# Two mixture-of-experts stages: index columns used where they lie, and two moved waits and reads

## The reference

```
# first experts: 8 experts, 256 hidden, the 2 best per token
topk_w, topk_idx = top_k(softmax(xf @ gate_w.T), 2)
for e in range(8):
    h = silu(xf @ w1[e].T) * (xf @ w3[e].T)
    out = out + gate_full[:, e:e + 1] * (h @ w2[e].T)

# second experts: 8 experts, 684 hidden, biases, the 2 farthest centroids
for e in range(8):
    h = silu(xs @ Wg[e] + bg[e]) * (xs @ W1[e] + b1[e])
    out = out + we[:, e:e + 1] * (h @ W2[e] + b2[e])
```

## Time and profile before

| | us |
|---|---|
| timed runs, median (lowest to highest) | 2411.94 (2408.89 to 2412.17) |
| the profiled execution's own time | 2414.36 |
| its span | 2412.6 |
| PE busy | 2079.7 (86%) |
| DVE busy | 1389.4 (58%) |
| ACT busy | 1534.8 (64%) |
| POOL busy | 440.3 (18%) |

### The profile page before, as it was taken

The page is one execution under the profiler, slowest core; times in us unless marked ns, Lnnn a source line. Parts: engine busy times, 40 slices in busy tenths (PEclk is TensorE's granted clock), DMA queues, the critical chain, the costliest instruction groups (busy, mean ns, idle before and its releaser), DMA issues. The chain is left out here.

```text
span 2412.6 us, 43912 instructions
## 1 busy us (share of the span) xinstructions
PE 2079.7 (86%) x13329; PEld 971.6 (40%) x13330; DVE 1389.4 (58%) x2986; ACT 1534.8 (64%) x2495; POOL 440.3 (18%) x678
## 2 busy tenths in 40 slices
PE   5997799950996999999999999999853699999992
PEld 4785455530661222222222222222242476766761
DVE  5567444347786444444445555553156687777774
ACT  2215333223774999999999999999862344444441
POOL 0030366642000000000000000000000134343430
PEclk9998899975996999999999999999976799999996
DMA  5001344443100000000002222222255265555656
GB/s 194 1 1 70 105 148 146 142 144 140 38 24 1 1 1 1 1 1 1 1 19 71 71 71 71 71 71 71 83 180 164 98 178 175 173 176 170 175 168 231
DMA packets 139075, 220.11 MB, mean 91 GB/s; under 512 B 14080, under 2 KB 108464, under 8 KB 138944
## 3 DMA queue, kind: packets, MB, share of 16 engines
q1 hardware_dynamic: 124160, 176.96, 23.6%
q0 software_dynamic: 13632, 37.24, 4.7%
q10 hardware_dynamic: 1152, 4.19, 0.4%
HBM read 161.82 MB, written 52.20 MB: 89 GB/s over the span
## 5 line engine op out<-in xcount | busy, mean ns | idle before, releaser
L1800 ACT ACTIVATE at_pexp<-at_psS 128x1024 f32<-128x1024 f32 x1024 | 964.2, 1023 | 42.9 <-PE at_psS L1706 39.8
L1814 DVE TENSOR_REDUCE at_mx<-at_psM 128x1 f32<-128x512 f32 x474 | 327.5, 691 | 464.3 <-PE at_psM L1733 464.3
L1720 PE MATMUL at_psO<-at_pexp,at_vst 128*32 128x512 f32 x4096 | 546.4, 605 | 0.1
L1706 PE MATMUL at_psS<-l1c_QT,l1c_KT 64*128 64x512 f16 x2048 | 403.6, 387 | 14.4 <-issue 5.6
L1706 PEld LDWEIGHTS at_psS<-l1c_QT,l1c_KT 64*128 64x128 f16 x2048 | 99.4, 92 | 632.4 <-ACT at_pexp L1800 598.9
L2136 PE MATMUL ex_psH<-wide_wgu,ex_xT 128*128 x1278 | 259.9, 357 | 0.2 <-issue 0.2
L2207 DVE SCALAR_TENSOR_TENSOR ex_bias<-ex_psH,top_w_scale,ex_bias 128x456 f32<-128x456 f32 x213 | 147.4, 692 | 76.7 <-PE ex_psH L2136 63.8
L988 POOL DMA_INDIRECT expert_rows<-ex_y,ex_odx x142 | 140.3, 988 | 259.5 <-issue 181.3
L2180 ACT ACTIVATE ex_sg<-ex_bias 128x228 f32<-128x228 f32 x213 | 83.7, 393 | 152.1 <-DVE ex_bias L2207 152.1
L1733 PE MATMUL at_psM<-at_ksumT,l1c_QT 64*128 64x512 bf16 x474 | 179.1, 378 | 0.6
L2136 PEld LDWEIGHTS ex_psH<-wide_wgu,ex_xT 128*128 128x128 f16 x1278 | 124.5, 97 | 111.8 <-issue 3.6
(11 more groups left out here) (362 smaller groups left out, 2782.6 us busy)
## 6 DMA issues: line engine op xcount, KB each, us to landing
ex_bias<-in_L_ffn_bg SPq DMA_DIRECT2D x71, 342.0 KB
ex_bias<-in_L_ffn_b SPq DMA_DIRECT2D x71, 342.0 KB
ex_piece<-in_L_ffn_W SPq DMA_DIRECT2D x48, 228.0 KB, 2.6
l1c_KT<-in_L_ffn_W SPq DMA_DIRECT2D x32, 342.0 KB, 3.4
halves<-l1c_KT SPq DMA_DIRECT2D x32, 342.0 KB, 3.3
wide_wgu<-halves SPq DMA_DIRECT2D x8, 1368.0 KB
ex_b<-in_L_ffn_b SPq DMA_DIRECT2D x71, 128.0 KB
normed<-rt_area SPq DMA_DIRECT2D x16, 512.0 KB, 2.6
```

Of the source, the lines that this page charges most:

```text
L1706: mm = pe.matmul(psS[:, n, hh * BANK:(hh + 1) * BANK], keys(k.KT, p)[r, kt * P:(kt + 1) * P], keys(k.QT, p)[r, c * BANK:(c + 1) * BANK], s ...
L1720: mm = pe.matmul(psO[g * VW:(g + 1) * VW, y, :], vst[:, p % 2, hh, kt, :], pexp[:, (p * ST + step) % 3 * 2 + n, hh * BANK:(hh + 1) * BANK] ...
L1800: act.activation(pexp[:, u % 6, :], psS[:, u % 2, :], ACT.Exp, scale=D ** -0.5 / (QS * QS)).then_inc(raised, 1)
L1814: dve.tensor_reduce(mx[:, n:n + 1], psM[:, :], AX.X, ALU.max).then_inc(reduced, 1)
```

## The change

Three edits. In `slot_transfers`, for both expert stages, the copies of index columns, the tiles idx and odx and the semaphores `indexed` and `passed` go; the transfers take their indices from the columns of `tok` and `dst`, and the 71 tiles are written as straight code. In the second experts SP waits, before it issues the biases of tile 0 and of tile 1, until the gather of that tile has landed. In the first experts PE's two reads of expert numbers move from the places where the numbers are used to the top of each step, ahead of the wait for the gather.

```diff
-    for st in steps(pool, NTILE, 8, LAG):
-        if st.on(0):
-            t, g = st.tile(0), st.slot(0, GR)
-            st.again(pool, got[g], st.lap(0, GR) * 16)
-            st.again(pool, x_turned, t - GR + 1)
-            pool.tensor_copy(idx[:, g, :], k.tok[:, ds(t, 1)]).then_inc(indexed, 1)
-        if st.on(LAG):
-            t, j = st.tile(LAG), st.slot(LAG, 2)
-            st.again(pool, put[j], st.lap(LAG, 2) * 16)
-            pool.tensor_copy(odx[:, j, :], k.dst[:, ds(t, 1)]).then_inc(indexed, 1)
...
-        if st.on(0):
-            pool.wait_ge(indexed, count)
-            pool.sem_inc(passed, 1)
+    for at in range(NTILE + LAG):
+        if at < NTILE:
+            t, g = at, at % GR
+            if t >= GR:
+                pool.wait_ge(got[g], t // GR * 16)
+                pool.wait_ge(x_turned, t - GR + 1)
             pool.indirect_dma_start(xg[:, g, :], None, k.xn_d,
-                                    bass.IndirectOffsetOnAxis(idx[:, g, :], 0)).then_inc(got[g], 16)
-        if st.on(LAG):
-            pool.wait_ge(indexed, count)
+                                    bass.IndirectOffsetOnAxis(k.tok[:, t:t + 1].bitcast(U32), 0)).then_inc(got[g], 16)
+        if at >= LAG:
+            t, j = at - LAG, at % 2
+            if t >= 2:
+                pool.wait_ge(put[j], t // 2 * 16)
             pool.wait_ge(y_done, t + 1)
-            pool.sem_inc(passed, 1)
-            pool.indirect_dma_start(k.y_d, bass.IndirectOffsetOnAxis(odx[:, j, :], 0), y[:, j, :],
+            pool.indirect_dma_start(k.y_d, bass.IndirectOffsetOnAxis(k.dst[:, t:t + 1].bitcast(U32), 0), y[:, j, :],
                                     None).then_inc(put[j], 16)
...
 (experts0, tensor)
                 for st in steps(pe, NTILE, 8, 3):
+                    eh, ey = (pe.value_load(k.tile_expert[0:1, ds(st.tile(lag), 1)], min_val=0, max_val=E - 1)
+                              if st.on(lag) else None for lag in (1, 3))
                     if st.on(0):
...
-                        e = pe.value_load(k.tile_expert[0:1, ds(t, 1)], min_val=0, max_val=E - 1)
                         pe.wait_ge(x_out, t + 1)
...
 (experts1, sync)
                         e = sp.value_load(k.tile_expert[0:1, ds(t, 1)], min_val=0, max_val=E - 1)

+                        if isinstance(t, int) and t < BR:
+                            sp.wait_ge(got[t], 16)
                         st.again(sp, h_done, (t - BR + 1) * HG)
```

More of the change, by code:

```diff
@@ L954, in _, with slot_transfers @@
                 ser(dve.tensor_scalar(k.tok[:, :], k.dst[:, :], T - 1, None, ALU.bitwise_and))
-def slot_transfers(pool, k, idx, odx, xg, y, got, put, x_turned, y_done, indexed, passed):
+def slot_transfers(pool, k, xg, y, got, put, x_turned, y_done):
     LAG = GR + 2
-    for st in steps(pool, NTILE, 8, LAG):
-        if st.on(0):
-            t, g = st.tile(0), st.slot(0, GR)
-            st.again(pool, got[g], st.lap(0, GR) * 16)
-            st.again(pool, x_turned, t - GR + 1)
-            pool.tensor_copy(idx[:, g, :], k.tok[:, ds(t, 1)]).then_inc(indexed, 1)
-        if st.on(LAG):
-            t, j = st.tile(LAG), st.slot(LAG, 2)
-            st.again(pool, put[j], st.lap(LAG, 2) * 16)
-            pool.tensor_copy(odx[:, j, :], k.dst[:, ds(t, 1)]).then_inc(indexed, 1)
[L975 to L978, removed]
-        if st.on(0):
-            pool.wait_ge(indexed, count)
-            pool.sem_inc(passed, 1)
-            pool.indirect_dma_start(xg[:, g, :], None, k.xn_d,
-                                    bass.IndirectOffsetOnAxis(idx[:, g, :], 0)).then_inc(got[g], 16)
-        if st.on(LAG):
-            pool.wait_ge(indexed, count)
+    for at in range(NTILE + LAG):
[4 more added lines that the diff above has]
+                pool.wait_ge(x_turned, t - GR + 1)
+            pool.indirect_dma_start(xg[:, g, :], None, k.xn_d,
+                                    bass.IndirectOffsetOnAxis(k.tok[:, t:t + 1].bitcast(U32), 0)).then_inc(got[g], 16)
[3 more added lines that the diff above has]
+                pool.wait_ge(put[j], t // 2 * 16)
             pool.wait_ge(y_done, t + 1)
-            pool.sem_inc(passed, 1)
-            pool.indirect_dma_start(k.y_d, bass.IndirectOffsetOnAxis(odx[:, j, :], 0), y[:, j, :],
+            pool.indirect_dma_start(k.y_d, bass.IndirectOffsetOnAxis(k.dst[:, t:t + 1].bitcast(U32), 0), y[:, j, :],
                                     None).then_inc(put[j], 16)
@@ L996, in experts0 @@
     with Stage(nc, "ex0") as s:
-        idx, odx = s.sb("idx", [P, GR, 1], U32), s.sb("odx", [P, 2, 1], U32)
         xg = s.sb("xg", [P, GR, C])
@@ L1011, in experts0 @@
         got, put = s.sems("got", GR), s.sems("put", 2)
-        indexed, passed = s.sem("indexed"), s.sem("passed")
         AR = 4
@@ L1039, in _ @@
             def _(pool):
-                slot_transfers(pool, k, idx, odx, xg, y, got, put, x_turned, y_done, indexed, passed)
+                slot_transfers(pool, k, xg, y, got, put, x_turned, y_done)
             @block.tensor
@@ L1061, in _ @@
                             mm = pe.matmul(psH[:, j, :], xT[:, j, kk, :],
-                                           k.w13[:, ds(e, 1), kk, :].rearrange("p a c -> p (a c)"),
+                                           k.w13[:, ds(eh, 1), kk, :].rearrange("p a c -> p (a c)"),
                                            start=(kk == 0), stop=(kk == KC - 1))
@@ L1079, in _ @@
                             mm = pe.matmul(psY[:, j, 0:C], hT[:, j, kk, :],
-                                           k.w2[:, ds(e, 1), kk, :].rearrange("p a c -> p (a c)"),
+                                           k.w2[:, ds(ey, 1), kk, :].rearrange("p a c -> p (a c)"),
                                            start=(kk == 0), stop=(kk == KC - 1))
```

## The result

The changed kernel takes 2392.57 us (median of 4 runs, 2387.68 to 2395.45) against 2411.18 us (4 runs of before beside it): a ratio of 0.9922, 95% interval 0.9904 to 0.9940. That is 18.6 us less. The prediction was 30.7 us less, 2382 us; the measured time lies within its range of 2375 to 2396, but outside the likeliest case's own, 2376 to 2390. The gain is six tenths of the one forecast. One of the forecast's own signs of being wrong also came up: the first stage was to be at least 17 us shorter, and it is 12.1 us shorter.

What follows compares the result with a forecast made beforehand. GpSimd's queue of index copies and indirect transfers was taken to bound the first experts, PE the second. Savings 22.8 + 1.5 + 0.7 + 5.7 = 30.7 us gave 2382 us, range 2375 to 2396.

Steps and rivals of the forecast that it cites:

- likeliest case: Whole kernel: the forecast's own case, 2382 us, with its own range 2376 to 2390 and a chance of 68%.
- signs of being wrong: Forecast wrong if the first stage is not at least 17 us shorter or the second start gains under 2 us.
- GpSimd's queue bounded the first experts: First experts: index copies and indirect transfers set the 3.40 us tile; without copies the round is 2.58 us (2.29 to 3.07).
- 22.8 us for the steady tiles: First experts, 62 periods: reads hidden, every tile falls from 3.40 to 3.03 us, saving 22.8 us.
- The reads' place: First experts: reads at the top are hidden, giving tiles of 3.03 us (22.8 us saved); with 3.12 it is 17.2.
- Rival 1: First experts: both reads exposed, array runs dry at each tile; tile 3.43 us, 2404 us in all; chance 8%.
- rival 4: First experts: another wait comes up, such as y for its buffer's last put; tile 3.13 to 3.31, 2388 to 2399 us; 8%.
- rival 2: Second experts' start: late biases hold DVE's add and eat the gain, up to 3.7 us more, about 2386 us; chance 10%.
- rival 3: First experts: the 0.79 us gap belongs to any transfer with its own waits; round 3.56 us, 2416 us; chance 6%.
- The start and the tail of the first experts: First experts: first psH matmul 1.5 us sooner (bounds 0.3 and 2); last put gains 0.7 us.
- The second start: Second experts: biases wait for first gathers, psH 6.2 us sooner, 0.5 taken off; gain 5.7 us (bounds 2 and 7).
- Straight code on GpSimd: GpSimd's loop of 8 tiles becomes straight code; cost taken as nothing, with 0.45 us per tile to spare.

Runs made afterwards that it cites:

- h first: DVE multiplies h of a tile before scaling y of an older one, first experts: 2380.09 us on the changed kernel, 2409.77 us on the kernel before.
- no reads: Changed kernel with PE's matmuls of the first experts all using expert 0's weights and reading no expert number; output differs from the reference: 2379.49 us.

## Why the prediction was right, and where its size was off

**Right: GpSimd's queue bounded the first experts.** With the copies gone the round could be 0.97 + 0.30 + 0.99 + 0.30 = 2.56 us, and the tile fell to 3.25 by the transfers alone; as long as the copies are there, neither the reads nor h first change anything.

**The term that was mis-sized: 22.8 us for the steady tiles, measured 10.3** (210.67 us for 62 periods before, 200.39 after). The step that failed is "DVE's h releases the h transposes about 1.0 us into the tile, the psY instructions follow within 0.3, the two reads end at 2.5, and the array wants the next transposes at 3.03. So the reads should vanish". Measured in the tile that starts at 379.11: h ends at 1.22, the two reads take the queue from about 1.6 to 3.0, and the transposes start at 3.24. Three small errors add up to 0.5 us, the whole slack: h 0.2 later, 0.1 more up to the first read, and 1.4 us instead of 1.2 for the two reads. Of each read, the load takes 0.30 and one register operation 0.15 us. By themselves these would just have fitted. But the sum ends where the reads end, and the 0.2 us from there to the start of the transposes had no term in it.

The sum also started from a favourable tile. Its 1.0 us fits one tile of 3.03 us of the kernel before, the one at 286.70, where h ends 1.02 us into the tile; in the next it ends at 1.24:

```profile
287.31 0.41 DVE L1120 TENSOR_TENSOR ex_h<-ex_psH,ex_sg 128x256 f32<-128x256 f32 x1
...
290.56 0.41 DVE L1120 TENSOR_TENSOR ex_h<-ex_psH,ex_sg 128x256 f32<-128x256 f32 x1
```

From there up to 390 us it ends 1.10 us or later in every tile of the kernel before, and so it does from tile 8 on in the changed one, except behind a jump, where the transposes themselves are late (0.7). The reason is the order on DVE: h stands behind y, and y behind the end of psY, the last matmuls ahead of the tile's transposes. That closes a ring through PE's queue, which the sum walked only in part. The two experiments that shorten this ring at different links (no reads, h first) both reach 3.03, and the one without GpSimd's relief reaches nothing.

The Trainium skill ("DMA: Bandwidth & Descriptors", latency and other measured facts) gives a floor of about 600 ns for a load into a register; two of them would be 1.2 us, an estimate from that page. In this case's traces the load instruction itself takes 0.30 us, half of that floor; with the register operation, the check and the gaps one read holds the queue about 0.7 us, 1.4 for the two.

**Also short: a jump in the loop.** The prediction gave it no term. At a lead of 0.25 us it costs 0.5: a tile of 3.7 us instead of about 3.2. With h first, at a lead of 0.8, the tile at the jump takes 3.10 to 3.12 us instead of 3.03. Over the 62 periods the six jumps account for some 3 of the 12.5 us by which the steady tiles fell short.

**The reads' place: credited with up to 5.6 us, worth little.** The prediction read the tiles of 3.12 us as the cost of the reads' old places (22.8 against 17.2 us). With the reads back there 62 tiles of the changed kernel take 201.6 us instead of 200.4, and the medians differ by 2.1 us, which can't be told from nothing; nor can the gain of the move in the kernel before.

**The rivals.** Rival 1, the exposed reads, named the mechanism that came true but priced it at a tile of 3.43 and 2404 us; rival 4 had the tile (3.13 to 3.31) and the time (2388 to 2399) with another cause. So the time lies inside the range because that was drawn to take in rival 2 and most of rival 4, and not because the forecast's own case held in the first experts; to that extent it was luck. Rival 4's example, y waiting for its buffer's last put, ended only 2.5 us of DVE's waits before y between 300 and 480 us; psY ended the rest. The 2.5 us are one wait, in the tile from 456.88 to 460.69, the one of 3.81 us without a jump:

```profile
L1117 DVE TENSOR_SCALAR ex_y<-ex_psY,top_wgt 128x256 f32<-128x256 f32 x55 | 26.6, 483 | 103.2 <-PE ex_psY L1066 100.7 <-DMA expert_rows<-ex_y,top_dst 2.5
...
457.87 0.48 DVE L1117 TENSOR_SCALAR ex_y<-ex_psY,top_wgt 128x256 f32<-128x256 f32 x1 [2.47 <-DMA expert_rows<-ex_y,top_dst]
```

**Right: rival 3 is false.** A transfer with waits of its own starts 0.30 us behind another when what it waits for is done. The 0.79 us of the old gathers stood behind a semaphore that the copy had only just raised, and a put stands as long behind a y just written (380.00 to 380.79). No run has the copies without that wait, or GpSimd's old loop without the copies, so how the gain divides between them isn't shown.

**The start and the tail of the first experts.** The second gather and the first psH matmuls:

```profile
263.67 0.95 POOL L969 DMA_INDIRECT ex_xg<-normed,top_tok  x1 [0.31 <-issue]
...
269.43 3.62 PE L1049 MATMUL ex_psH<-l_w,ex_xT 128*128 x4
```

psH starts 9.2 us behind `top_tok` instead of 10.3: 1.1 gained of the 1.5 forecast. Half of that is gone by tile 8, since the ring already slows the first tiles, which ran at 3.03 to 3.12 before: tile 8 is 0.5 us sooner. From tile 70's transposes to the last put it is now 503.39 - 492.19 = 11.2 us against 12.5, 1.3 gained where 0.7 was forecast:

```profile
502.14 0.48 DVE L1117 TENSOR_SCALAR ex_y<-ex_psY,top_wgt 128x256 f32<-128x256 f32 x1 [1.02 <-DMA expert_rows<-ex_y,top_dst]
...
503.39 0.97 POOL L977 DMA_INDIRECT expert_rows<-ex_y,top_dst  x1 [0.53 <-issue]
```

In sum 0.5 + 10.3 + 1.3 = 12.1 us, the gain of the stage.

**The second start: forecast 5.7, measured 6.5 to 6.6.** Its steps held. The gathers landed in 3 us, psH started 7.0 us sooner (forecast 6.2), DVE's add waited for a bias pair that took 1900.06 - 1893.26 = 6.8 us (the 6.7 of the earlier trace rows), and 0.5 was given back. What was better is the first gather. With no copy ahead it starts 1.97 us behind `top_tok` instead of 2.74, 0.8 sooner where I had given it 0.3. Rival 2, the late biases, would have cost up to 3.7 us.

**Straight code on GpSimd** shows no cost: its transfers start 0.30 us behind one another or wait for DVE.

## What to carry to other kernels

When a queue that sets a loop's period is relieved, the next period is not the busy time of the next engine but the longest ring of waits through all of them; walk that ring once with every queue instruction and every older instruction that stands ahead on an in-order engine, and take the start times in it from several tiles, not from one (here 1.02 in one tile, 1.24 in the next, and the slack was 0.5). On an engine in the ring, let the instruction that releases the critical one go first (here h before y), even at the price of another step of depth; in the profiled first stage that was worth 12.2 us, unrolling the loop 6.3 and moving the reads 1.4. An edit that gains nothing while one bound stands may be worth most once it is gone, so try it again then.

## What the runs showed of the hardware

- An indirect transfer on GpSimd starts 0.30 us behind another indirect transfer, whether gather or put came first, if what it waits for is done by then. It starts 0.78 to 0.79 us behind the instruction that it waits for when that ends last, be it a copy of its own engine or DVE's y. The two copies of 0.19 us each and this wait made the round 3.39 us, where it can be 2.56 without them.
- With four bias transfers of 342 KB in flight the first gathers land after 7.3 to 8.1 us, against 2.8 in the quiet loop, and they then hold the whole start. With the biases held back the first gather's transposes start 3.0 us after it does. A pair of bias transfers takes 6.8 us up to its use, 6.7 before.
- A number read from on-chip memory into a register of PE's queue takes 0.30 us for the load alone, about 0.65 to 0.7 with what follows it up to the check. Two of them were hidden in a tile of 3.03 us when the h that they wait behind ended 0.46 us into the tile, and not when it ended at 1.22.
